# One launch of two layers on one core: attention by query block, with layer 0's other products laid between its steps

## What is computed

```python
xn = _layernorm(x)
# branch 1, 16 heads of 64: keys and values are projections of 32 chunk means
summary = chunk means of xn; q = xn @ Wq + bq; k, v = summary @ Wk + bk, summary @ Wv + bv
a = softmax(where(chunk end <= position, q k^T / 8, -inf)) v @ Wo + bo
# branch 2, 16 query heads and 4 key heads of 8
h = rmsnorm(xn); q, k, v = rope and rmsnorm of h @ Wq, h @ Wk; h @ Wv
out = softmax(causal(q k^T / sqrt(8))) v
out = out * sigmoid(out @ Wg + bg)
m = xn + out @ Wo + bo
h2 = rmsnorm(m); top1 = argmax(h2 @ Wr + br)
b = m + expert(top1)(h2)          # 8 experts, u1 * sigmoid(u2), 256 wide
x = x + a + b
```

## Time and profile before

| | us |
|---|---|
| median of 3 runs (lowest to highest) | 768.86 (767.79 to 769.92) |
| the profiled execution, its time | 767.02 |
| its span, first to last instruction | 765.1 |
| PE, ACT, DVE, POOL busy | 640.9, 471.6, 386.5, 209.1 |

### The profile page before, as it was taken

The page is one execution under the profiler, slowest core; times in us unless marked ns, Lnnn a source line. Parts: engine busy times, 40 slices in busy tenths (PEclk is TensorE's granted clock), DMA queues, the critical chain, the costliest instruction groups (busy, mean ns, idle before and its releaser), DMA issues.

```text
span 765.1 us, 11411 instructions
## 1 busy us (share of the span) xinstructions
PE 640.9 (84%) x4134; PEld 388.6 (51%) x4134; DVE 386.5 (51%) x873; ACT 471.6 (62%) x671; POOL 209.1 (27%) x234
## 2 busy tenths in 40 slices
PE   3568999999999999999844159965897999999997
PEld 2554333334333333333334037754785778878786
DVE  7988344134414441333196413336646656666763
ACT  1124688968898889898753114452664766666663
POOL 3003333143205331523058610017010223122231
PEclk9655699989999999999975559985999999999999
DMA  6940000000000000000225120011000000000000
GB/s 191 87 1 1 1 1 1 1 1 1 1 1 2 1 2 1 1 1 2 77 92 183 42 93 28 18 40 49 3 1 0 1 1 15 1 15 1 1 15 15
DMA packets 29159, 18.92 MB, mean 25 GB/s; under 512 B 8704, under 2 KB 25368, under 8 KB 29104
## 3 DMA queue, kind: packets, MB, share of 16 engines
q1 hardware_dynamic: 28080, 16.08, 10.3%
q0 software_dynamic: 1024, 2.10, 0.9%
HBM read 13.06 MB, written 5.13 MB: 24 GB/s over the span
## 4 chain that ended last, share of the span: by engine, by line
PE 56%; DVE 19%; ACT 14%; issue 8%; POOL 3%; DMA 1%; SPq 0%; ACTq 0%; DVEq 0%; POOLq 0%
PE ps L1104 14%; PE ps L1088 8%; ACT r L791 5%; PE ps L86 4%; PE ps L88 3%; PE ps L87 3%; PE ps L1122 2%; POOL rows_by_expert L722 2%; PE ps L1335 2%; DVE r L1832 2%; PE ps L1132 1%; PE ps L1119 1%; DVE r L1614 1%; PE ps L1114 1%; PE ps L1197 1%
## 5 line engine op out<-in xcount | busy, mean ns | idle before, releaser
L791 ACT ACTIVATE r<-ps 128x1024 f32<-128x1024 f32 (+3 forms) x320 | 260.3, 924 | 46.8 <-PE ps L1088 45.9
L1104 PE MATMUL ps<-r 128*32 128x512 f32 (+3 forms) x1280 | 155.5, 559 | 4.5 <-DVE r L1544 2.7
L699 POOL TENSOR_TENSOR r<-r,consts 128x256 f32<-128x256 f32 x128 | 93.4, 746 | 218.7 <-ACT r L791 218.5
L1088 PE MATMUL ps<-r2r 32*128 32x512 f32 (+3 forms) x640 | 100.9, 475 | 6.8 <-ACT r L791 5.4
L1088 PEld LDWEIGHTS ps<-r2r 32*128 32x128 f32 x640 | 44.3, 188 | 94.0 <-issue 46.4
L748 POOL TENSOR_TENSOR r<-r 128x512 f32<-128x512 f32 x16 | 23.6, 1473 | 142.3 <-ACT r L972 142.3
L1104 PEld LDWEIGHTS ps<-r 128*32 128x32 f32 x1280 | 25.6, 109 | 41.1 <-issue 23.4
L87 PE MATMUL ps<-r2r 128*128 128x512 f32 (+1 forms) x96 | 37.2, 388 | 0.0
L727 POOL DMA_INDIRECT r<-expert_rows,r x16 | 16.4, 1025 | 74.9 <-DMA expert_rows<-r 70.3
L1544 DVE COPY r<-ps 128x512 f32<-128x512 f32 x16 | 11.0, 685 | 50.5 <-PE ps L1104 50.5
L972 ACT ACTIVATE r<-r 128x512 f32<-128x512 f32 x16 | 10.1, 632 | 34.3 <-DVE r L1832 34.3
(11 more groups left out here) (346 smaller groups left out, 1407.9 us busy)
## 6 DMA issues: line engine op xcount, KB each, us to landing
r<-in_f_W SPq DMA_DIRECT2D x1, 2048.0 KB, 9.3
rows_by_expert<-r SPq DMA_DIRECT2D x1, 1472.0 KB, 13.6
expert_rows<-r SPq DMA_DIRECT2D x5, 256.0 KB, 2.2
res<-in_x SPq DMA_DIRECT2D x4, 256.0 KB, 3.6
r<-in_g_h1T SPq DMA_DIRECT2D x1, 1024.0 KB, 5.8
r<-in_g_h2T SPq DMA_DIRECT2D x1, 1024.0 KB, 8.0
r<-rows_by_expert SPq DMA_DIRECT2D x2, 512.0 KB, 4.3
out<-res SPq DMA_DIRECT2D x4, 256.0 KB, 2.3
```

The lines of the kernel that those rows point to most:

```text
L699: pool.tensor_tensor(blk, blk, along(tri, 2), ALU.mult).then_inc(s_msk, 1)
L791: act.activation(probs[:, n % PBUFS, :, off:TB], ps[:, b:b + 2, off:TB], ACT.Exp).then_inc(s_exp, 1)
L1088: m = pe.matmul(ps[:, 2 * (n % SBUFS) + h, off:TB], kst[32 * j:32 * j + 32, g, P * kt:P * kt + P], qst[32 * j:32 * j + 32, g, qb * TB + of ...
L1104: m = pe.matmul(ps[32 * j:32 * j + 32, 6, off:TB], vp[:, kt, g, :], probs[:, (2 * v + j // 2) % PBUFS, j % 2, off:TB], start=(v == FIRST[n ...
```

## The change

- `BLOCKS` goes by query block first, then key head. Only token block 0's queries and keys are made before the loop. Queries are transposed four heads at a time with high and low parts already doubled in `qhl`, so the selector products for queries are gone. Keys are transposed once per token block (`keysT`); for block 0 four selector products spread them, for blocks 1 to 3 sixteen DMAs from the SP queue do (`spread_keys`).
- Two key heads share one accumulator (`PAIRED`): `vp` holds the values of odd heads nine columns further, so bank 6 is copied and transposed 8 times instead of 16.
- Side work is planned by `ASKED` with an earliest step, a number of parts (a part a step), a predecessor and a gap; a greedy loop gives each step at most one part. New items: QKV for blocks 2 and 3, KV, GMAT, G0, VW (the summary products), and a chain OT, GATE, WO, XT, LOGITS for each token block as soon as its attention is done. By the plan 93 of 99 items end within the 160 steps; ATT and the chain of block 3 stand behind them.
- The summary probabilities are stored compactly (only the chunks that a block can see), so TRANSPOSE and OUTPUT take m+1 products instead of 4 for token block m. The matching rows of `vw` are regrouped through DRAM.
- The gate's sigmoid is a tanh, with `wo` and `bgc` halved. The router is applied to the rows before their scaling and scaled afterwards, mean squares come from bn_stats, and `h2` itself is written after the one-hot steps, before the slots.
- PBUFS is 6 instead of 8. Expert weights and layer 1's weights are loaded earlier. Some buffers move.

With `events` on DVE new kinds: 4 (square sums and values of block 2 or 3, after QKV), 5 (rotation and split), 6 (bias additions), 7 (gating), 8 (chunk means), 9 (tables of the router). The core of the diff:

```diff
-SBUFS, PBUFS = 3, 8
+SBUFS, PBUFS = 3, 6
...
-        BLOCKS = [(g, qb, kt, max(0, kt - TPB * qb) * P) for g in range(NKV) for qb in range(NB)
+        BLOCKS = [(g, qb, kt, max(0, kt - TPB * qb) * P) for qb in range(NB) for g in range(NKV)
...
+        PAIRED = [(a, qb) for qb in range(NB) for a in range(NKV // 2)]
+        FIRST = {(a, qb): of_round(2 * a, qb)[0] for a, qb in PAIRED}
+        LAST = {(a, qb): of_round(2 * a + 1, qb)[-1] for a, qb in PAIRED}
+        BEGIN = [of_round(0, qb)[0] for qb in range(NB)]
+        END = [of_round(NKV - 1, qb)[-1] for qb in range(NB)]
...
+        CHAIN = (("OT", 1, 0), ("GATE", 1, 2), ("WO", 2, 3), ("XT", 1, 2), ("LOGITS", 1, 2))
+        CHAIN_FROM = (64, 88, 118, 0)
+        ASKED = sorted(
+            [(at + 2 * n, 2, "QKV", (b, n), None, 0) for b, at in ((2, 10), (3, 16)) for n in range(2)]
+            + [(7, 1, "KEYS", 1, None, 0)]
+            + [(at, 1, "KEYS", b, ("QUERIES", (b - 1, NKV - 1)), gap) for b, at, gap in ((2, 30, 7), (3, 74, 12))]
+            + [(at, 2, "QUERIES", (b, g), ("KEYS", b), 1) for b, steps in
+               ((1, (8, 14, 20, 22)), (2, (41, 44, 58, 66)), (3, (87, 99, 112, 128))) for g, at in enumerate(steps)]
+            + [(24, 6, "KV", 0, None, 0), (32, 6, "GMAT", 0, ("KV", 0), 1), (41, 6, "G0", 0, ("KV", 0), 1),
+               (48, 4, "VW", 0, ("KV", 0), 1)]
+            + [(LAST[r] + LAG + 1, 2, "ATT", r, None, 0) for r in PAIRED]
+            + [(54 + 6 * u, 1, "SCORE", u, ("TRANSPOSE", u - 2) if u > 1 else ("VW", 0), 1) for u in range(NT)]
+            + [(54 + 6 * u, 1, "TRANSPOSE", u, ("SCORE", u), 4) for u in range(NT)]
+            + [(54 + 6 * u, 1, "OUTPUT", u, ("TRANSPOSE", u), 1) for u in range(NT)]
+            + [(at, parts, what, b, (CHAIN[n - 1][0], b) if n else ("ATT", (1, b)), gap)
+               for b, at in enumerate(CHAIN_FROM) for n, (what, parts, gap) in enumerate(CHAIN)],
+            key=lambda e: e[0])
+        AUX, ended, at = [], {}, 0
+        while len(AUX) < len(ASKED):
+            ready = [e for e in ASKED if e[2:4] not in ended and e[0] <= at
+                     and (e[4] is None or e[4] in ended and ended[e[4]] + e[5] <= at)]
+            if ready:
+                _, parts, what, which, _, _ = ready[0]
+                AUX.append((range(at, at + parts), what, which))
+                ended[what, which] = at + parts - 1
+                at += parts
...
+        SUMM_EXP = {aux_end("SCORE", u) + 2: u for u in range(NT)}
+        TANH_AT = {aux_end('GATE', b) + 1: b for b in range(NB)}
+        ROOT_AT = aux_end("QKV", (3, 1)) + 3
...
-            sp.wait_ge(s_pv, len(BLOCKS))
+            def spread_keys(b):
+                sp.wait_ge(s_kc, b + 1)
+                for g in range(NKV):
+                    for j in range(REP):
+                        sp.dma_start(kst[32 * j:32 * j + 32, g, b * TB:b * TB + TB].bitcast(F32),
+                                     keysT[32 * g:32 * g + 32, :].bitcast(F32)).then_inc(s_krep, 16)
...
+            spread_keys(3)
+            sp.wait_ge(s_krep, 16 * NQ * (NB - 1))
+            sp.wait_ge(s_split, NB)
+            sp.wait_ge(s_mr, aux_index["QUERIES", (NB - 1, NKV - 1)] + 1)
             sp.dma_start(w1, io["f_W1"].rearrange("e p f -> p e f")).then_inc(s_moew, 16)
+            sp.wait_ge(s_mr, aux_index["SCORE", NT - 1] + 1)
             sp.dma_start(w2, io["f_W2"].rearrange("e (c p) d -> p e c d", p=P)).then_inc(s_moew, 16)
+
+            sp.wait_ge(s_pv, STEPS)
...
-            pool.wait_ge(s_ss2, NB)
+            pool.wait_ge(s_biasw, 16 * 6)
             step.alone(pool.memset(biases, 0.0))
-            pool.wait_ge(s_biasw, 16 * 6)
...
+            pool.wait_ge(s_h2, 1)
...
+                if b < 2:
+                    act.wait_ge(s_qkvc, TPB * (b + 1))
+                    act.activation(sq, qkv[:, b, :, 0:160], ACT.Square).then_inc(s_sq, 1)
+                    act.wait_ge(s_ssq, b + 1)
+                    act.activation(rr[:, b], ssq[:, b], ACT.Sqrt, bias=RMS_EPS, scale=1.0 / QD).then_inc(s_qksd, 1)
...
+                if k in TANH_AT:
+                    act.wait_ge(s_mf, aux_index["GATE", TANH_AT[k]] + 1)
+                    act.activation(gate, ps[:, SHARED, :], ACT.Tanh, bias=bgc, scale=0.5).then_inc(s_mr, 1)
...
+                act.wait_ge(s_pv, STEPS)
                 act.activation(hi, w, ACT.Copy).then_inc(s_whi, 1)
 
-            act.wait_ge(s_ss2, NB)
-            act.activation(sdm, ssq2, ACT.Sqrt, bias=RMS_EPS, scale=1.0 / D).then_inc(s_sd2, 1)
             weights_high(0)
-            for b in range(NB):
-                act.wait_ge(s_h2T, b + 1)
-                act.activation(h2T[:, b * TB:b * TB + TB], ps[:, b, :], ACT.Copy, scale=ln2).then_inc(s_h2Tc, 1)
+            act.wait_ge(s_var, 3)
+            act.activation(sdm, ms2, ACT.Sqrt, bias=RMS_EPS).then_inc(s_sd2, 1)
...
+            for b in range(2):
+                normed_transposed(b)
...
+            pe.wait_ge(s_split, 1)
+            pe.wait_ge(s_qkvc, 2 * TPB)
+            pe.wait_ge(s_xnTc, NB)
+            keys_transposed(7).then_inc(s_kt, 1)
+            queries_transposed(0, 0).then_inc(s_sqt, 1)
+            pe.wait_ge(s_kc, 1)
             pe.wait_ge(s_sel, 1)
-            for b in range(NB):
-                pe.wait_ge(s_kac, b + 1)
-                keys_spread(4 + b, 0, b).then_inc(s_skt, 1)
-            for b in range(NB):
-                pe.wait_ge(s_qac, b + 1)
-                queries_spread(b, 0, b).then_inc(s_sqt, 1)
-            for b in range(NB):
-                pe.wait_ge(s_skc, b + 1)
-                queries_transposed(4 + b, 1, b).then_inc(s_qbt, 1)
-
-            pe.wait_ge(s_qbc, NB)
-            pe.wait_ge(s_pad, 2)
-            pe.wait_ge(s_vp, 2)
-            pe.wait_ge(s_sqc, NB)
-            for step_ in range(len(BLOCKS) + LAG + 3):
-                if step_ < len(BLOCKS):
-                    g, qb, kt, off = BLOCKS[step_]
-                    if g:
-                        pe.wait_ge(s_mr, aux_index["KEYS", (g, kt // TPB)] + 1)
-                        pe.wait_ge(s_mr, aux_index["QUERIES", (g, qb)] + 1)
-                    for n in (2 * step_, 2 * step_ + 1):
+            for g in range(NKV):
+                at = slice(32 * g, 32 * g + 32)
+                pe.matmul(ps[:, 2 * g + 1, :], selk[at, :], keysT[at, :], start=True, stop=True).then_inc(s_skt, 1)
+                if g + 1 < NKV:
+                    queries_transposed(2 * g + 2, g + 1).then_inc(s_sqt, 1)
...
+                for n, what, which, part, parts in AUX_AT.get(k, ()):
+                    if n and not part:
                         pe.wait_ge(s_mr, n)
-                    if what == "SCORE":
+                    elif not part:
+                        pe.wait_ge(s_skv, 2)
...
+                    elif what == "KEYS":
+                        pe.wait_ge(s_split, which + 1)
+                        a = keys_transposed(SHARED)
+                    elif what == "QUERIES":
+                        a = queries_transposed(SHARED, which[1], share(TPB))
...
+                        for q in range(m + 1):
+                            a = pe.matmul(ps[:, SHARED, 0:D], ptr[:, P * q:P * q + P], vws[m][:, q, :],
+                                          start=(q == 0), stop=(q == m))
...
+            def split(b):
+                flat = rot.rearrange("p i h d -> p (i h) d")
+                step.alone(dve.reciprocal(ssq[:, b], rr[:, b]))
+                step.alone(dve.tensor_tensor(flat, flat, over(ssq[:, b], QD), ALU.mult))
+                kr, qr = rot[:, :, NQ:20, :], rot[:, :, 0:NQ, :]
+                step.alone(dve.tensor_tensor(kr, kr, kw.unsqueeze(1).unsqueeze(1).broadcast_to([P, TPB, NKV, QD]),
...
+            for b in range(2):
+                for i in range(TPB):
+                    dve.wait_ge(s_qkvp, TPB * b + i - i % 2 + 2)
+                    qkv_taken(b, i, ps[:, 4 + 2 * b + i // 2, (i % 2) * QKV_W:(i % 2) * QKV_W + QKV_W]
+                              ).then_inc(s_qkvc, 1)
+                if b == 0:
+                    normed(2)
+                    normed(3)
+                dve.wait_ge(s_sq, b + 1)
+                squares_summed(b)
+                dve.wait_ge(s_qkvc, TPB * (b + 1))
+                values_placed(b)
+                if b == 0:
+                    dve.wait_ge(s_ssq, 1)
+                    rotated(0)
+                    dve.wait_ge(s_qksd, 1)
+                    split(0)
...
+                if kind == 5:
+                    rotated(n)
+                    dve.wait_ge(s_qksd, 3)
+                    dve.wait_ge(s_mr, aux_index["QUERIES", (n - 1, NKV - 1)] + 1)
+                    split(n)
...
+                    for odd in range(2):
+                        step.mark(dve.reciprocal(rden[:, odd, 0:NQ], src[:, :, (QD + 1) * odd + QD]))
+                    step.settle()
...
+                    dve.tensor_tensor(blk, blk, bank.rearrange("p (i d) -> p i d", d=D), ALU.add).then_inc(s_mr, 1)
+                    dve.wait_ge(s_mr, n + 1)
```

(18 more changed lines are left out.)

818 lines of the change are left out of this document (425 added, 393 removed).

## The result

The changed kernel takes 749.55 us (median of 4 runs, 745.72 to 751.52), the kernel before in the same session 769.39 (767.79 to 770.37): ratio 0.974, interval 0.969 to 0.978. It is faster, by 20 us instead of the forecast 48, and lies outside the range of 704 to 738. The profiled execution took 750.56, with a span of 748.8.

What follows compares the result with a forecast made beforehand. VectorE bounds the prologue, ScalarE and PE nearly fill attention, a VectorE/GpSimd chain follows. Gains of 27.7, 11.2 and 9.4 us, 48.4 in all, gave span 716.7 and time 720.5 us; range 704 to 738.

Steps and rivals of the forecast that it cites:

- Prologue: Before the loop: first score product at 39.5 us instead of 67.2, a gain of 27.7 us.
- Block 0: First 16 value products, all diagonal: 30 us (27 to 33), GpSimd's masks the bound once PE is fast.
- PBUFS: Loop: six buffers instead of eight cost nothing; if the cover fails, 0.3 us a step.
- keys late: Rival, chance 0.10: a block waits for DMAs spreading its keys, some 2 us at each of three boundaries; 726 us.
- factor 1.05: Loop, blocks 1 to 3: allowance over the summed bounds, giving 263 us; 3 us of stall lie in it.
- sum of the blocks' larger bounds: Loop: per query block the larger of PE's and ScalarE's work, 51.5, 82.8 and 116, adding to 250.3 us.
- the rival with 1.09: Loop hardly tighter than the old one, chance 0.20: 10 us more, 730.5 us.
- The stall at step 72: Loop: block 3's rotation and split on VectorE delay freeing the shared bank for WO and SCORE; 3 us of stall.
- slower: Rival, chance 0.02: loop items wait on VectorE and stop scores; decides at 0.52 us an item, 786 us at 0.7.
- From the loop to the experts: Last value product to expert start: GpSimd's line is the later one, 62.9 us against 72.3, a gain of 9.4.
- h2 scalings: Behind the loop on VectorE: sixteen come behind GpSimd's subtractions by the port lock, 16 x 0.27 = 4.3 us, before the slots.
- The rest: Experts and layer 1, where only addresses change: 316.4 us, as before.

Runs made afterwards that it cites:

- e12: The fine pieces kernel (e9) with the summary attention's TRANSPOSE and OUTPUT items cut to one product each; 727.53 us, ratio .944 to the kernel before.
- e9: Fine pieces: changed kernel, two free steps behind GATE and KV, rotation and split of blocks 2, 3 in six pieces, bias additions in four; 733.83 us, ratio .956.
- e7: Changed kernel with the three weight subtractions behind the loop moved from GpSimd to VectorE, behind the slot chain; 744.99 us, ratio .965 to the kernel before.
- e11: The changed kernel run once more, unedited, for its time and a second profile; 746.55 us, ratio .973 to the kernel before.

## Why the prediction was wrong, and where it was right

**Prologue: right.** 39.82 for 39.5, with VectorE busy 27.74 of it. The gain of 27.4 us is the largest of the change.

**Block 0: the number right, the reason not borne out.** 30.1 for 30. GpSimd's masks were to be the bound with value products waiting for them. GpSimd was busy 26.45 of 34.22 us, PE 30.79, at a mean granted clock of 0.83, and PE waited for masks 0.9 us in all. PE's granted clock was 0.58 up to 50.0, 0.83 up to 60.0 and 1.00 behind that, where PE was still busy 12.7 of 14.0 us. So PE, first at its low level and then with its side items, looks like what set this pace; no run tests it, and the hit is luck in part.

**PBUFS and keys by DMA.** No row shows a new wait for either but 0.91 us before the scores at 70.21, so the rival "keys late" is out at 2 us a boundary. PBUFS was not tried by itself.

**Loop: the step that failed is the factor 1.05 on the sum of the blocks' larger bounds.** 250.3 became 293.5 for the three blocks, 1.17; even the rival with 1.09 was too mild. The runs and rows split these 43 us:

- 5 us: PE's own work. By start-to-start times of the fine pieces' trace it is 53.8, 83.3 and 118.1 us, 255.2 against 250.3.
- 15 us: the larger of two engines was taken per block, but three score buffers even it out only within about a step. Taken step by step (ScalarE 1.83, PE 1.43 plus the item, less in diagonal blocks) the larger ones add to 56.8 + 87.7 + 124.6 = 269.1, and the last value product takes 1.1 more. This is worked out; that it is the right account is borne out by e12 (block 3 forecast to fall 6.2 by it, fell 5.6) and by the 2.52 us step above, not proved. It depends on which exponential is set beside which step of PE: moved by one or two steps, the same prices add to 266 to 276, so this part and the short waits below can't be told apart to better than some 6 us.
- 2.4 us: two table loads in block 1, shown by two runs. The prediction counted those leaving the tail and overlooked the two that the root brings into the loop.
- About 4 us: short waits that remain in e9 (276.3 in all, to the end of the last).
- 17 us: long waits, 293.5 less 276.3, which fine pieces and free steps removed; up to 3.4 of them are the clock's chance in block 1 (1.5 at 24 to 27, 2.0 at 32 to 35). They are the held bank and accumulator behind VectorE's long pieces and behind the tanh, with the low clock after them. By the granted means of 0.90 and 0.95 PE stood at the low level for some 23 us of blocks 1 and 2. Its busy time for the same products in the three blocks was 274.3 us in the change and 266.5 in the fine pieces. So up to 8 of the 17 us are slower products, and the rest is waiting.

The factor had room for 12.7 us of all this. The stall at step 72 was forecast in place and cause, at 3 us; fine pieces and the free steps took 7.4 us off value products 68 to 75. What the prediction missed is that the 5 to 8 us pieces cost at every place where they stood: block 2's rotation with the bias addition behind it, at 28 to 35, cost about as much. The rival "slower" had this very mechanism, a late release stopping scores through PE's order; at 30.5/93 = 0.33 us an item beyond forecast it stayed under its deciding point of 0.52.

**From the loop to the experts: the sum right, by terms that cancel.** The subtractions ended at 394.5, +27.0 instead of +30.4 (the bias split began at +3.3, 370.80, instead of +4.5, and took 10.1 us instead of 11.6; the recorded sum at T+16.7 has 0.6 us more than its terms); VectorE then took 8.5 us to the scatter instead of 7.1, which came at +35.5 instead of +37.5; and from the scatter to the expert start it was 27.2 us instead of 25.4, 1.4 of it the slow issue at 404.55 (2.44 us against 1.01 before). So +62.7 for 62.9 is luck in its last 2 us; the mechanism, GpSimd's line as the late one with VectorE's steps held behind it, is right. The h2 scalings came behind GpSimd's work as assumed, but were not themselves held: 3.20 us for sixteen. What was held are the two-input steps ahead of them. e7 shows the cause by taking it away. By the rule of the Trainium skill that the prediction weighed (SBUF — State Buffer, Who interferes with whom), that is the exclusive port lock; the traces agree for the two-input operations. Whether GpSimd's slow scatter issues beside VectorE's large operations are the same thing from the other side, no run here took apart.

**The rest.** 318.6 for 316.4. The unedited change took 315.5 us there in its second profile (e11), and runs with the same code from there on 315.4 to 321.9, so the 2 us are no effect of the change that can be read.
